# Gate and up projections as Strassen block products over two weight blocks and two token groups

## The reference

```python
x = _layernorm(x + attention(x, Wq, Wk, Wv, Wo))
x = _layernorm(x + experts(x, itok, ctx, ctx, ctx))
h = silu(x @ w_gate) * (x @ w_up)          # 2048 tokens, 512 -> 2048
h = _sparsify_2to4(h)                      # of each 4 neighbours keep the 2 of largest magnitude
x = _layernorm(x + h @ w_down)             # 2048 -> 512
```

## Time and profile before

| | us |
|---|---|
| median of 3 runs | 1091.44 (1091.35 to 1092.93) |
| profiled execution, span | 1090.9 |
| attention and experts, up to the first gate matmul | 548.9 |
| feed-forward part, up to the last up matmul | 510.8 |
| tail behind it | 31.2 |

### The profile page before, as it was taken

How to read it: one execution, slowest core, us unless ns; L and a number is a source line. 1 busy time by engine, 2 the same in 40 slices (tenths; PEclk the granted TensorE clock), 3 DMA queues, 4 the chain that set the end, 5 groups by cost and what they waited for, 6 DMA issues and landing times.

```text
span 1090.9 us, 18063 instructions
## 1 busy us (share of the span) xinstructions
PE 1037.0 (95%) x6022; PEld 839.6 (77%) x6023; DVE 738.5 (68%) x1769; ACT 486.3 (45%) x905; POOL 294.7 (27%) x496
## 2 busy tenths in 40 slices
PE   7889998999999885999999999999999999999996
PEld 6667776777777664888888888888888888888885
DVE  5898699778868986566747546545565536654666
ACT  5688488758857884222324222131222122221124
POOL 2186348545733641223210006000000000000224
PEclk9999999999999998999999999999999999999998
DMA  8877267727743732224541003210020000100102
...
DMA packets 55216, 106.18 MB, mean 97 GB/s; under 512 B 6240, under 2 KB 8288, under 8 KB 55136
## 3 DMA queue, kind: packets, MB, share of 16 engines
...
...
## 4 chain that ended last, share of the span: by engine, by line
PE 57%; DVE 2%; ACT 1%; issue 0%; DMA 0%; POOL 0%; POOLq 0%; DVEq 0%
PE f_bank L53 55%; PE f_bank L1714 1%; PE f_bank L1722 1%; PE f_bank L1793 1%; PE f_bank L1738 0%; DVE ln_stats L1104 0%; DVE rows_kept L2150 0%; ACT rows_kept L1132 0%; DVE h L2116 0%; DMA rows<-sorted_dram 0%; DVE rows_kept L2139 0%; DVE h L2056 0%; DVE rows_kept L1111 0%; POOL out L1660 0%; ACT fsg L1936 0%
## 5 line engine op out<-in xcount | busy, mean ns | idle before, releaser
L1896 ACT ACTIVATE fsg<-f_bank 128x512 f32<-128x512 f32 x64 | 38.2, 598 | 295.6 <-PE f_bank L53 289.2
L2056 DVE TENSOR_TENSOR h<-f_bank,fsg 128x512 f32<-128x512 f32 x64 | 44.2, 691 | 181.6 <-PE f_bank L53 181.4
L714 ACT ACTIVATE probs<-bank,nmax 128x384 f32<-128x384 f32 (+3 forms) x256 | 131.7, 549 | 21.4 <-DVE nmax L899 19.3
L883 DVE CUSTOM_DVE_ANT_0 bank<-bank,mask 128x384 f32<-128x384 f32 (+3 forms) x256 | 122.9, 502 | 13.8 <-PE bank L510 13.0
L521 PE MATMUL bank<-ident,probs 128*128 128x128 f32 x640 | 108.7, 284 | 24.6 <-DVE pt_lo L908 10.7
L1137 POOL TENSOR_SCALAR ln_var<-ln_mv 128x1 f32<-128x1 f32 x39 | 8.9, 229 | 438.8 <-DVE ln_mv L1106 437.4
L908 DVE TENSOR_TENSOR pt_lo<-bank,pt_hi 128x512 f16<-128x512 f32 (+1 forms) x192 | 114.7, 598 | 16.7 <-ACT pt_hi L724 16.4
L724 ACT ACTIVATE pt_hi<-bank 128x512 f16<-128x512 f32 (+1 forms) x192 | 104.9, 546 | 23.5 <-PE bank L521 22.9
L53 PE MATMUL bank<-x_hi,w_qk 128*128 128x512 f32 x256 | 101.5, 414 | 6.7 <-DVE x_lo L913 6.3
L53 PE MATMUL f_bank<-wd_hi,hs_lo 128*128 128x512 f32 x256 | 100.0, 391 | 0.0
L53 PE MATMUL f_bank<-wd_lo,hs_hi 128*128 128x512 f32 x256 | 99.9, 390 | 0.0
...
## 6 DMA issues: line engine op xcount, KB each, us to landing
...
```

The lines of the kernel that those rows point to most:

```text
L714: ins = act.activation(probs[u % RP][:, at:at + cols(r)], S[u % SR][:, at:at + cols(r)], ACT.Exp, bias=nmax[:, r, c:c + 1])
L883: dve.tensor_tensor_reduce(out=S[u % SR][:, at:at + cols(r)], in0=S[u % SR][:, at:at + cols(r)], in1=mask[:, T - cols(r):T], scale=1.0, sc ...
L1896: act.activation(fsg[v % 2][:, :], GB[v % 2][:, :], ACT.Silu).then_inc(s_sg, 1)
L2056: dve.tensor_tensor(h[r % 2][:, j, :], UB[v % 2][:, :], fsg[v % 2][:, :], ALU.mult).then_inc(s_h, 1)
```

## The change

Tokens are taken in pairs of groups (pass 0: groups 0 and 1, pass 1: groups 2 and 3), passes outermost. With gate and up as two weight blocks, the width of 512 cut in two halves of 256 and two token groups, each column block is a 2 x 2 by 2 x 2 block product. It is made of 7 block products for 8, of 6 matmuls each (2 steps of 128 rows x 3 parts), `m1` to `m7`. That makes U = 32 groups `group(g)`, g = 4k + j: k is the round (a chunk in a pass, k = 0 to 7), j the column block.

- **Weight sums** S1 to S4 are made by GpSimd for each group (`weight_sums`, four operations of 128x256), and GpSimd also makes all low parts (`gate_lo` 128x512, `sums_lo` 128x768, `up_lo` and `fourth_lo` 128x256). ScalarE makes the high parts. Gate and up weights are loaded, summed and cut once in each pass.
- **Token differences** T1 to T4 are made by GpSimd from `x2` (128x1024 each, into `t_rows` and `t_more`), then turned by PE (`turn_piece`) and cut.
- **Results.** m1, m6, m7 and m4 add into one bank (`AB`), and ScalarE copies its state behind m1 (`copy1`, into g0), behind m6 (`copy2`, into g1) and behind m7 (`copy3`, into v1). VectorE adds m2 to g0 (`c11`), m5 to v1 (`c22`), m3 to g1 (`c12`). `silu0` and `silu1` act on g0 and g1. VectorE multiplies for the first token group (`product0`), GpSimd for the second (`product1`).
- **Order on PE**: m1(g), m2(g), m4(g-1), down tiles, m6(g), m3(g-1), m5(g), down tiles, m7(g). Down tiles of a round stand 2, 4 and 2 in the groups j = 2, j = 3 and j = 0 that follow, none in j = 1. Three banks take turns for them; the last 12 tiles stand behind the last product.
- **Order on the others**: compare, count and choose of a round lie in the groups of the next one (`compare_fourth` and `count_wins` of token group 0 and its `choose` at j = 0, both `kept_lo` and `compare_three` of group 1 at j = 1, the rest of group 1 at j = 2 and 3).
- **Moved**: GpSimd's token scatters go into the expert tiles, `write` of the first pass's tiles into groups 26 to 31, their `rstd` behind `product1` of groups 24 and 28, their `normed_early` (ScalarE) into groups 25 and 29.
- **Tail**: both token groups of the last round go through in halves, four in all.

```diff
-            def inner(c, v):
-                r, j = v // J, v % J
-                n = c * NR * J + v
-                for m, (w, banks, s_read, s_done) in enumerate(((wg, GB, s_sg, s_g), (wu, UB, s_h, s_u))):
-                    if r == 0:
-                        pe.wait_ge(s_pl, PIECES * c + 2 * j + m + 1)
-                    if later(n, 2):
-                        pe.wait_ge(s_read, n - 1)
-                    matmul3(pe, banks[v % 2][:, :], lambda k, i: w[i][:, j, k, :],
-                            lambda k, i: hs[i][:, k, :] if first and r == 0 else xt[i][:, k, r * TW:(r + 1) * TW],
-                            KT).then_inc(s_done, 1)
...
-                        outer(*before(c, v, 1))
...
+        AB, BB, CB, YB = [bank[2], bank[4]], bank[3], bank[0:2], [bank[5], bank[7], bank[6]]
...
+            def weight_sums(u):
+                pool.tensor_tensor(s_raw[:, 0], w[:, 0:2], w[:, 2:4], ALU.add).then_inc(s_sum, 1)
+                pool.tensor_tensor(s_raw[:, 2], g[:, 0:2], w[:, 0:2], ALU.subtract).then_inc(s_sum, 1)
+                pool.wait_ge(s_sum, 4 * u + 1)
+                pool.tensor_tensor(s_raw[:, 1], s_raw[:, 0], g[:, 0:2], ALU.subtract).then_inc(s_sum, 1)
+                pool.wait_ge(s_sum, 4 * u + 3)
+                if u >= 1:
+                    pool.wait_ge(s_wl, 4 * u)
+                pool.tensor_tensor(s_raw[:, 3], g[:, 2:4], s_raw[:, 1], ALU.subtract).then_inc(s_sum, 1)
...
+            def gate_lo(u):
+                i = u % 2
+                pool.wait_ge(s_wh, 4 * u + 1)
+                pool.wait_ge(s_sum, 4 * u + 4)
+                pool.tensor_tensor(w_lo[i][:, G01:G23 + 1].rearrange("p a k n -> p (a k) n"), m.gate_raw[i][:, :, :],
+                                   w_hi[i][:, G01:G23 + 1].rearrange("p a k n -> p (a k) n").bitcast(F32),
+                                   ALU.subtract).then_inc(s_wl, 1)
...
+            def product1(u):
+                k, j = u // J, u % J
+                pool.wait_ge(s_sg1, u + 1)
+                if k > 0 and j >= 2:
+                    pool.wait_ge(s_hl, 4 * k)
+                pool.tensor_tensor(h[1][:, at_slot(k, j), :], v1[u % 2][:, :], g1[u % 2][:, :],
+                                   ALU.mult).then_inc(s_h1, 1)
...
+            def group(g):
+                if g == MID:
+                    rows_turned(1, T2)
+                    pool.tensor_tensor(t_rows[:, :, :], half_rows(3, 0), half_rows(2, 0), ALU.subtract).then_inc(s_trows, 1)
+                up_lo(g)
+                fourth_lo(g)
+                if g + 1 < U:
+                    weight_sums(g + 1)
+                    gate_lo(g + 1)
...
+                if g + 1 < U:
+                    sums_lo(g + 1)
+                if g >= 1:
+                    product1(g - 1)
...
+            def product(out, u, w, x, first=True):
+                chain = [(k, a, b) for k in range(2) for a, b in ((0, 0), (0, 1), (1, 0))]
+                for n, (k, a, b) in enumerate(chain):
+                    ins = pe.matmul(out[:, :], (w_hi, w_lo)[a][u % 2][:, w, k, :], piece(x, k)[b],
+                                    start=(first and n == 0), stop=(n == len(chain) - 1), skip_group_check=not first)
+                ins.then_inc(s_prod, 1)
...
+            def m2(u):
+                if u >= 1:
+                    pe.wait_ge(s_sum_up, c11_count(u - 1))
+                turned_in(u, B21)
+                product(BB, u, G23, B21)
...
+            def m4(u):
+                pe.wait_ge(s_wl, 4 * u + 3)
+                pe.wait_ge(s_copy, 3 * u + 3)
+                turned_in(u, T4)
+                product(AB[u % 2], u, U23, T4, False)
+            def m3(u):
+                pe.wait_ge(s_wl, 4 * u + 4)
+                pe.wait_ge(s_sum_up, c22_count(u))
+                turned_in(u, B22)
+                product(CB[u % 2], u, S4, B22, False)
...
+            def group(g):
+                m1(g)
+                m2(g)
...
+                if g >= 1 and g != MID + 1:
+                    m4(g - 1)
+                for y_tile in outers(g, 0):
+                    outer(*y_tile)
+                m6(g)
...
+                else:
+                    if g >= 1:
+                        m3(g - 1)
+                    m5(g)
+                for y_tile in outers(g, 1):
+                    outer(*y_tile)
+                m7(g)
...
+            def sums_hi(u):
+                i = u % 2
+                act.wait_ge(s_sum, 4 * u + 3)
+                if u >= 2:
+                    act.wait_ge(s_prod, nth(7, u - 2))
+                act.activation(w_hi[i][:, S1:S3 + 1], s_raw[:, 0:3], ACT.Copy).then_inc(s_wh, 1)
...
+            def copy3(u):
+                act.wait_ge(s_prod, nth(7, u))
+                if u >= 2:
+                    act.wait_ge(s_h1, u - 1)
+                act.activation(v1[u % 2][:, :], AB[u % 2][:, :], ACT.Copy).then_inc(s_copy, 1)
...
+            def group(g):
+                k, j = g // J, g % J
+                if g >= 1:
+                    copy3(g - 1)
...
+                    up_hi(g)
+                    fourth_hi(g)
+                    if g + 1 < U:
+                        gate_hi(g + 1)
+                    copy1(g)
+                    if g + 1 < U:
+                        sums_hi(g + 1)
...
+                    if j == 1 and k >= 1:
+                        magnitudes(k - 1)
+                    if j == 3 and k >= 1:
+                        kept_hi(k - 1, 1, 0)
+                    silu0(g)
+                if j == 0 and k >= 1:
+                    fourth_magnitude(k - 1, 0)
+                copy2(g)
...
+                if j == 1 and k >= 1:
+                    for half in range(2):
+                        kept_hi(k - 1, 0, half)
+                if j == 3 and 1 <= k < NK - 1:
+                    kept_hi(k - 1, 1, 1)
+                silu1(g - 1)
+                if j == 1 and k >= 1:
+                    down_hi(k - 1)
+                if j == 3:
+                    first_magnitudes(k, 0)
+                if g in (25, 29):
+                    first = g - 25
+                    for t in range(first, first + RW):
+                        normed_early(t)
...
+            def c12(u):
+                dve.wait_ge(s_prod, nth(3, u))
+                dve.wait_ge(s_copy, 3 * u + 2)
+                dve.tensor_tensor(g1[u % 2][:, :], CB[u % 2][:, :], g1[u % 2][:, :], ALU.add).then_inc(s_sum_up, 1)
...
+            def group(g):
+                k, j = g // J, g % J
...
+                c22(g - 1)
+                if k >= 1 and j == 2:
+                    down_lo(k - 1, (0, 1))
+                if k >= 1 and j == 3:
+                    choose(k - 1, 1)
+                    for i in range(2):
+                        add_up(k - 1, i)
+                c11(g)
...
+                if k >= 1 and j == 2:
+                    down_lo(k - 1, (2, 3))
+                product0(g - 1)
+                if j == 0:
+                    for y_tile in outers(g, 0):
+                        add_up(*y_tile)
+                    if k >= 1:
+                        compare_fourth(k - 1, 0)
+                        count_wins(k - 1, 0)
+                if k >= 1 and j == 1:
+                    for half in range(2):
+                        kept_lo(k - 1, 0, half)
+                if k >= 1 and j == 2:
+                    compare_fourth(k - 1, 1)
+                    count_wins(k - 1, 1)
+                if k >= 1 and j == 3:
+                    for y_tile in outers(g, 0):
+                        add_up(*y_tile)
...
+                    kept_lo(k - 1, 1, 0)
+                c12(g - 1)
+                if j == 0 and k >= 1:
+                    choose(k - 1, 0)
+                if j == 1 and k >= 1:
+                    compare_three(k - 1, 1)
+                if j == 3:
+                    if 1 <= k < NK - 1:
+                        kept_lo(k - 1, 1, 1)
+                        for y_tile in outers(g, 1):
+                            add_up(*y_tile)
+                    compare_three(k, 0)
```

994 lines of the change are left out of this document (653 added, 341 removed).

## The result

The changed kernel takes **1209.93 us** (median of 4 runs, 1201.51 to 1211.93) against 1091.97 (1091.35 to 1092.93, 4 runs): ratio 1.107, 95% interval 1.103 to 1.110. I had forecast 1143.5 with a range of 1075 to 1168. The sign was right and the size was not: it is 66 us more than I said.

A forecast was written before the change was run, and what follows sets the result against it. PE's own work bounded the kernel; after the change waits would outweigh its gain: 1010.0 + 8 start + 6 middle + 17 LayerNorm + 51 rounds + 51 tail = 1143.0, plus 0.5 for the median: 1143.5 us, range 1075 to 1168.

The forecast's parts named there:

- A round costs 4.7 to 10.0, I take 7.3: Rounds k = 1 to 7: PE waits cost 7.3 us each, 51 us in all, bounds 33 and 70.
- The walk with VectorE and GpSimd taking turns: One round, VectorE's operations on two SBUF tiles not overlapping GpSimd's: losses 3.4, 3.3 and 3.3, 10.0 us a round.
- With GpSimd busy 27% of the span its slack hides the scatters: Expert tiles: 16 scatters moved there cost nothing; if that cover fails, 18 us, left to the range.
- Start 8, bounds 0 and 10: Group 0: PE, ready at 8.4 us, waits for T3's row difference behind GpSimd's queue; 8 us.
- In the middle 6, bounds 0 and 10: Middle: four row differences (9.6 us) and six converted pieces on the same queues, beside 15 us of PE work; 6 us.
- LayerNorm 17: Rounds 6 and 7: GpSimd's four rstd and ScalarE's four normed_early add 2 x 8.8 = 17 us, bounds 6 and 18.
- The clock: Feed-forward part: PE at a granted clock of 1.00, each matmul taken at 0.2265 us; no term for a lower clock.
- GpSimd's queue: Each group: GpSimd gets 8.4 us of work where PE has 9.5; the total fits, so queue order counts.
- Tail 51: Behind the last product: four halves where two followed before; 51 us in all, 20 more than before.
- The rival with heavy block: VectorE's and GpSimd's work also does not overlap with what each waits for: 16 us a round, 1204 us; chance 0.08.
- The rival PE-bound: Every copy comes in time, so rounds, start, middle and LayerNorm cost nothing: 1061 us, faster; chance 0.17.
- the rival without the block: Waits without VectorE-GpSimd blocking: 4.7 us a round, 1125 down to 1094; part of the forecast's case, which had 0.72.

The follow-up runs named there:

- the combined kernel: The changed kernel with the round edits, scatters later, start, LayerNorm spread and tail edits, without the middle group's earlier cut of turned rows; 1141.75 us, with GpSimd's weight work as constants 1088.96.

## Why the prediction was right and wrong

What failed is the size, 66 us, and four steps of the prediction make most of it: the cover that set the expert tiles to nothing, the two short walks of start and middle, and the missing clock. The points in turn:

- **The sign and its main cause: right.** Waits of PE through ScalarE's copies, and behind them GpSimd's `s_raw` and VectorE's `c12`, are what costs. The forecast marks are met: j = 1 of round 2 takes 12.8 us (12 to 13 said), `choose` takes 1.15 us in the mean, the six operations into `wins` 0.78, two of them 1.2, and GpSimd is busy 62% of the feed-forward part.
- **"A round costs 4.7 to 10.0, I take 7.3": right** for rounds 2 and 5 (7.8, 7.9), partly by luck. By quarter, round 2 loses 3.3, 3.2 and 1.3 us in j = 1, 2 and 3. The walk with VectorE and GpSimd taking turns said 3.4, 3.3 and 3.3, the one without 1.6, 3.1 and 0. So the walk with turns was the nearer one, and only its j = 3 was too dear. The waits in round 2 are 5.6 us, and matmuls at the lower clock behind them another 1.7, a cost that the walk did not have. Round 1 lost 12.1.
- **"With GpSimd busy 27% of the span its slack hides the scatters": wrong,** the largest plain error. The term was set to 0 and measures 17.0; without the scatters it is gone. The cover named was an engine's time, and the cost is in the DMA. The price that I left to the range, 18 (16 issues on GpSimd), met the 17 by chance; its mechanism was another.
- **"Start 8, bounds 0 and 10": mis-sized,** 22.7. The step had one wait, for T3. The trace has a first one of 6.0 for `t_more`, behind the scatter of tile 17, and the T3 wait was 10.4; with clock and cuts the rest. The forecast's own numbers, GpSimd done at 10 + 7.9 and PE ready at 8.4, give 9.5 and not 8. Experiment: 13.1 of it come off with an order.
- **"In the middle 6, bounds 0 and 10": mis-sized,** 21.6. I had counted GpSimd's 9.6 us of differences against 15 of PE, and not that the cuts of the turned pieces stand among VectorE's top-2 work (compare, count, choose) of those groups. PE waits 6.3 us for an `add_up` behind `choose` and 7.0 for a cut behind the counts. Beside the row differences VectorE's counts were stretched most, from 0.42 and 0.69 us (timeline of PE, then of VectorE):

```profile
868.90 1.12 PE L2055 MATMUL f_bank<-ident,rows_kept 128*128 128x128 f32 x4 [7.03 <-DVE xb_lo L2514]
```
```profile
860.36 2.59 DVE L2568 TENSOR_TENSOR wins<-beats 128x512 bf16<-128x512 bf16 x1
862.99 2.71 DVE L2570 TENSOR_TENSOR wins<-wins,beats 128x1024 bf16<-128x1024 bf16 x1
```

- **"LayerNorm 17": right as a price,** 16.1 by spreading it; but rounds 6 and 7 still lose 9.8 and 14.1 then, where the sum gave them 7.3 each.
- **The clock: a term put at nothing** without a word. The earlier trace rows showed 1.00, and the sum took 0.2265 us for every matmul. The 27 us at the lower level lie inside the measured terms.
- **GpSimd's queue: somewhat short.** The walk had 8.4 us a group; the means of its nine operations sum to 10.3. The 128x256 ones take 0.73 us undisturbed, as forecast, and 0.93 in the mean: GpSimd is stretched as well as VectorE.
- **"Tail 51": nearly right,** 55.5, of which 2.8 are the half copy behind the squares, which the walk missed.
- **The rival with heavy block, 1204 at 0.08,** came out by its number and not by its mechanism: rounds 2 and 5 lose 8, not 16. The rival PE-bound was only reached in the rounds, with GpSimd's weight work left out.
- **Slips that change little:** with its low ends the rival without the block comes to 1100, not 1094, since LayerNorm's low end of 6 was left out. The tail's terms sum to 32.3, not 32.6. And 45 matmuls in 10.23 us are 0.2273 each; 0.2265 is the spacing of most of them.

The deeper fault is the range. Of the four small terms (expert tiles, start, middle, LayerNorm), two went to more than twice their upper end of 10, and the others came to 17 and 25 where 18 was the end. I added their middles and ended the range at 1168. The upper ends of the prediction's own text sum to 1010 + 10 + 10 + 18 + 70 + 51 + 18 = 1187. That would have been the honest end, and even it was too low by the start, the middle and the lower clock. That one common cause made them all late is not shown: the scatters' cause is the DMA, and what the experiments took off came off side by side once the rounds were mended, 48 of 51 us.

**Still open:** what rounds 6 and 7 lose beside LayerNorm; why the combined kernel's middle is still 12 us over its share with GpSimd's work as constants (groups 15 to 17 62.5 us, some 50 of it PE's own work by my count); and whether the kernel with `product1` on VectorE, with its scatters held apart, would be the best one. Its groups 2 and 3 lost 11 us together, so by that estimate it could come to some 1116, still over the kernel before. This was not tried.
